# A float32 feature network on one core: six raw slots in place of four, six steps opened by halves, side work cut small

## The reference, cut to what matters

```python
# features (1024, 2, 5128), stm (1024, 2, 1), W_ft (512, 5128), b_ft (512,),
# W1 (32, 1024), b1 (32,), W2 (1, 32), b2 (1,), all float32
w = jnp.einsum('bpf,mf->bpm', features, W_ft) + b_ft
l1_x = jnp.clip(stm * w, 0.0, 1.0).reshape(features.shape[0], -1)
l2_x = jnp.clip(l1_x @ W1.T + b1, 0.0, 1.0)
return l2_x @ W2.T + b2
```

## Time and profile before

| | us |
|---|---|
| median of 3 runs | 432.38 |
| the three runs | 429.82, 432.38, 434.44 |
| the profiled execution, its own time | 432.02 |
| its span, first to last instruction | 430.2 |

### The profile page before, as it was taken

One profiled execution on the slowest core, in us unless ns is written; L12 is line 12 of the kernel. 1 busy time (PEld: TensorE's weight loads), 2 busy tenths in 40 slices (PEclk: granted clock), 3 DMA queues, 4 the chain that ended last, 5 costly groups with the idle time before them and its releaser, 6 DMA issues.

```text
span 430.2 us, 4578 instructions
## 1 busy us (share of the span) xinstructions
PE 407.0 (95%) x1756; PEld 323.3 (75%) x1756; DVE 349.6 (81%) x321; ACT 196.2 (46%) x176; POOL 13.2 (3%) x32
## 2 busy tenths in 40 slices
PE   6969999979999989998999999999999899999995
PEld 4747777858777868786878888878788778888862
DVE  3887888896899989979899877897887975698625
ACT  4464454343448444424444674363444448444300
POOL 2090000000000000000000000000000000000000
PEclk9999999989999999998999999999999999999999
DMA  7999797876867666663666766658667766778200
GB/s 237 387 239 269 219 267 247 253 226 200 264 227 244 223 233 235 244 226 143 244 245 244 240 222 237 240 205 337 239 235 238 240 194 195 240 231 254 96 2 0
DMA packets 27300, 96.37 MB, mean 224 GB/s; under 512 B 3432, under 2 KB 6384, under 8 KB 22032
## 3 DMA queue, kind: packets, MB, share of 16 engines
q1 hardware_dynamic: 26656, 95.44, 66.9%
q0 software_dynamic: 624, 0.66, 0.8%
HBM read 96.08 MB, written 0.00 MB: 223 GB/s over the span
## 4 chain that ended last, share of the span: by engine, by line
PE 65%; DMA 15%; DVE 12%; issue 5%; SPq 2%; ACT 1%; DVEq 0%
PE sums L496 63%; DMA xs<-x_p 15%; DVE x_lo L400 5%; DVE w_lo L397 1%; DVE xs L374 1%; PE sums L554 1%; PE sums L598 1%; DVE ws L378 1%; DVE x_lo L352 1%; DVE c_all L413 1%; ACT x_hi L275 0%; SPq L209 0%; DVE c_all L477 0%; DVE ws L364 0%; DVE xr L454 0%
## 5 line engine op out<-in xcount | busy, mean ns | idle before, releaser
L496 PE MATMUL sums<-x_lo,w_hi 128*128 128x512 f32 x560 | 178.0, 396 | 13.8 <-DVE x_lo L400 13.6
L496 PE MATMUL sums<-x_hi,w_hi 128*128 128x512 f32 x560 | 178.0, 396 | 3.2 <-ACT x_hi L264 2.3
L496 PE MATMUL sums<-x_hi,w_lo 128*128 128x512 f32 x560 | 177.2, 395 | 0.2 <-DVE w_lo L347 0.2
L289 ACT ACTIVATE x_hi<-xs 128x2048 fp32r<-128x2048 f32 x67 | 128.7, 1921 | 79.6 <-DVE xs L384 34.9
L400 DVE TENSOR_TENSOR x_lo<-xs,x_hi 128x2048 fp32r<-128x2048 f32 x67 | 153.0, 2284 | 0.0
L496 PEld LDWEIGHTS sums<-x_lo,w_hi 128*128 128x128 f32 x560 | 104.9, 190 | 42.2 <-issue 21.0
L496 PEld LDWEIGHTS sums<-x_hi,w_hi 128*128 128x128 f32 x560 | 106.4, 191 | 29.2 <-ACT x_hi L264 2.8
L496 PEld LDWEIGHTS sums<-x_hi,w_lo 128*128 128x128 f32 x560 | 106.8, 191 | 23.5 <-DVE w_lo L347 0.6
L284 ACT ACTIVATE w_hi<-ws 128x512 fp32r<-128x512 f32 x67 | 42.5, 634 | 116.9 <-PE sums L496 42.1
L397 DVE TENSOR_TENSOR w_lo<-ws,w_hi 128x512 fp32r<-128x512 f32 x67 | 45.9, 684 | 14.7 <-DMA ws<-w_p 14.7
L384 DVE TENSOR_TENSOR xs<-xs 128x2048 f32<-128x2048 f32 x20 | 45.8, 2288 | 8.0 <-DMA xs<-x_p 8.0
(11 more groups left out here) (59 smaller groups left out, 88.7 us busy)
## 6 DMA issues: line engine op xcount, KB each, us to landing
xs<-x_p SPq DMA_DIRECT2D x40, 1024.0 KB, 5.6
xs<-x_p SPq DMA_DIRECT2D x57, 512.0 KB, 5.6
ws<-w_p SPq DMA_DIRECT2D x43, 256.0 KB, 3.2
ws<-w_p SPq DMA_DIRECT2D x17, 384.0 KB, 3.4
ws<-w_p SPq DMA_DIRECT2D x20, 128.0 KB, 4.1
open_x<-x_p SPq DMA_DIRECT2D x2, 512.0 KB, 6.9
stm_all<-stm SPq DMA_DIRECT2D x1, 1024.0 KB, 7.5
open_x<-x_p SPq DMA_DIRECT2D x2, 256.0 KB, 3.8
```

Source lines behind the costliest of these rows:

```text
L289: nc.scalar.activation(x_hi[:, g % HI, :, :], x_pair(g), ACT.Copy).then_inc(x_hi_ready, 1)
L496: return nc.tensor.matmul(sums[:, bank, :], w[:, wslot, wpos, m * P:(m + 1) * P], x[:, xslot, xpos, c * BANK:(c + 1) * BANK], start=start, ...
```

## The change

- `RAW` 4 becomes 6. Slots 0 to 3 lie where they lay (`RAW_HOME`). Slots 4 and 5 of `xs` lie, until step 40 (`TURN`), in 4 x 4 KB per partition that later hold blocks 2 and 3 of `c_all` (`c_late`), and from step 40 on in the first four kept `x` blocks, whose last use is step 43. The raw area of `ws` shrinks from three to two blocks per slot, as the third block of pass 0 is now loaded straight to its kept place, by a DMA of its own (`s_loaded`).
- Loads of steps up to 39 and from 46 on wait for step g - 6; those of steps 40 to 43 for step g - 4 as before; those of 44 and 45 for `x_sum`, so for the kept blocks to have been read.
- `OPEN` 3 becomes 6: steps 3, 4 and 5 are also made by halves, from their normal slots; three steps are still staged (`STAGED`). Of the opening, `open_low(5, 2, 1)` moves ahead of `sums_of(3)`.
- `WARM_UP` 8 becomes 16.
- Rest: the two memsets and the small DMAs of POOL come after three steps in place of two (and none of the two memsets at the start); L454's two and L457 go from g = 12 to g = 12, 14 and 16.
- `combine` and the multiplications of `finish` go by 128x1024, at g = 45, 46, 48, 49 and 54, 55, with the clip at g = 57. In the fourth pass they are also cut, at the same g as before.

The core of the diff (renames and pure re-indexing left out):

```diff
-WARM_UP = 8
+WARM_UP = 16
-OPEN = 3
-RAW = 4
+STAGED = 3
+OPEN = 6
+RAW = 6
+RAW_HOME = 4
-OPEN_HALVES = ((0, 0), (1, 0), (0, 1), (2, 0), (1, 1), (2, 1))
+OPEN_HALVES = ((0, 0), (1, 0), (0, 1), (2, 0), (1, 1), (2, 1), (3, 0), (3, 1), (4, 0), (4, 1), (5, 0), (5, 1))
+TURN = 2 * K_PAIRS
...
+        c_early = sb("c_early", [P, 2, 2 * COLS])
+        c_late = sb("c_late", [P, 2, 2 * COLS], at=xs_at + 4 * CST * COLS)
...
+        def slot(g):
+            return g % RAW if g < TURN else (g - TURN) % RAW
+        def raw_x(g):
+            n = slot(g)
+            if n < RAW_HOME:
+                return 2 * n
+            return (CST if g < TURN else TST) + 2 * (n - RAW_HOME)
...
-            for g in range(OPEN, STEPS):
+            for g in range(STAGED, STEPS):
                 f, k = pass_of(g)
-                if g >= RAW:
+                if g in (TURN + RAW_HOME, TURN + RAW_HOME + 1):
+                    sp.wait_ge(x_sum, TURN + 2 * (g - TURN - RAW_HOME + 1))
+                elif TURN <= g < TURN + RAW_HOME:
+                    sp.wait_ge(step_done, g - RAW_HOME + 1)
+                elif g >= RAW:
                     sp.wait_ge(step_done, g - RAW + 1)
                 if f == 0:
-                    sp.dma_start(ws[:, i:i + 3, :], w_p[k, :, 0:3, :]).then_inc(w_loaded[n], 16)
+                    sp.dma_start(ws[:, i:i + 2, :], w_p[k, :, 0:2, :]).then_inc(w_loaded[n], 16)
+                    sp.dma_start(ws[:, KEPT + k, :], w_p[k, :, 2, :]).then_inc(s_loaded[n], 16)
...
-            pool.memset(xr_raw[:, :], 0.0).then_inc(rest_zeroed, 1)
-            pool.memset(wr_raw[:, :, :], 0.0).then_inc(rest_zeroed, 1)
...
-            pool.wait_ge(step_done, 2)
+            pool.wait_ge(step_done, STAGED)
+            pool.memset(xr_raw[:, :], 0.0).then_inc(rest_zeroed, 1)
+            pool.memset(wr_raw[:, :, :], 0.0).then_inc(rest_zeroed, 1)
...
             def open_half(n, g, pos):
+                if g >= HI:
+                    sc.wait_ge(step_done, g - HI + 1)
...
                 if g == K_PAIRS + 2:
+                    sc.wait_ge(rest_ready, 3)
                     drain(0)
...
             sums_of(2)
+            open_low(5, 2, 1)
+            for g in range(STAGED, OPEN):
+                sums_of(g)
+                open_low(2 * g, g, 0)
+                open_low(2 * g + 1, g, 1)
             sums_of(OPEN)
-            open_low(5, 2, 1)
...
-                if g == third + 5:
-                    combine(3, c_all[:, 2, :], 1, 16)
-                if g == third + 8:
-                    dve.wait_ge(c_sum, 1)
-                    combine(3, c_all[:, 1, :], 2, 16)
-                if g == third + 16:
-                    finish(3, 1, 2)
+                for m in range(2):
+                    cols = slice(m * COLS, (m + 1) * COLS)
+                    if g == TURN + 5 + m:
+                        combine(3, m, c_all[2][:, cols], 16)
+                    if g == TURN + 8 + m:
+                        dve.wait_ge(c_sum, m + 1)
+                        combine(3, m, c_all[1][:, cols], 16)
+                    if g == TURN + 14 + m:
+                        scale(3, 1, m, m + 3)
+                if g == TURN + 17:
+                    clip(3, 6)
```

More of the change, by code:

```diff
@@ L114, in feature_net @@
         t_loaded = [sem(f"t_loaded{j}") for j in range(RAW)]
-        open_w_loaded = [sem(f"open_w_loaded{j}") for j in range(OPEN)]
-        open_x_loaded = [sem(f"open_x_loaded{j}") for j in range(OPEN + 1)]
+        s_loaded = [sem(f"s_loaded{j}") for j in range(RAW)]
+        open_w_loaded = [sem(f"open_w_loaded{j}") for j in range(STAGED)]
+        open_x_loaded = [sem(f"open_x_loaded{j}") for j in range(STAGED + 1)]
         open_hi = sem("open_hi")
@@ L351, in open_low @@
                     dve.wait_ge(open_hi, before + 2 + i)
-                    nc.vector.tensor_tensor(x_lo[:, g, pos, a:b], x_src[:, a:b],
-                                            x_hi[:, g, pos, a:b].bitcast(F32), ALU.subtract)\
+                    nc.vector.tensor_tensor(low_x(g)[:, pos, a:b], x_src[:, a:b],
+                                            x_hi[:, g % HI, pos, a:b].bitcast(F32), ALU.subtract)\
                         .then_inc(open_lo, 1)
@@ L466, in _ @@
+                if g == TURN + 17:
+                    clip(3, 6)
                 if g == fourth + 2:
-                    combine(1, xs[:, TST:TST + 2, :].rearrange("p m n -> p (m n)"), 5, 24)
+                    for m in range(2):
+                        combine(1, m, xs[:, OUT + m, :], 24)
                 if g == fourth + 3:
-                    finish(1, 1, 5)
+                    for m in range(2):
+                        scale(1, 1, m, m + 7)
+                    clip(1, 10)
                 if g == fourth + 4:
-                    combine(2, xs[:, TST + 2:TST + 4, :].rearrange("p m n -> p (m n)"), 8, 24)
+                    for m in range(2):
+                        combine(2, m, xs[:, OUT + 2 + m, :], 24)
@@ L472, in _ @@
                 if g == fourth + 5:
-                    finish(2, 0, 8)
+                    for m in range(2):
+                        scale(2, 0, m, m + 11)
+                    clip(2, 14)
             for b in range(4):
@@ L494, in _, with product, operands @@
         def _(pe):
-            def product(bank, w, wslot, wpos, x, xslot, xpos, m, c, start, stop=False):
-                return nc.tensor.matmul(sums[:, bank, :], w[:, wslot, wpos, m * P:(m + 1) * P],
-                                        x[:, xslot, xpos, c * BANK:(c + 1) * BANK], start=start, stop=stop,
-                                        skip_group_check=True)
+            def product(bank, w, x, m, c, start, stop=False):
+                return nc.tensor.matmul(sums[:, bank, :], w[:, m * P:(m + 1) * P], x[:, c * BANK:(c + 1) * BANK],
+                                        start=start, stop=stop, skip_group_check=True)
+            def operands(g, wpos, xpos):
+                return (w_hi[:, g % HI, wpos, :], w_lo[:, slot(g), wpos, :],
+                        x_hi[:, g % HI, xpos, :], low_x(g)[:, xpos, :])
             def open_products(n, g, pos):
@@ L506, in open_products @@
                         for m in range(2):
-                            product(m * 2 + c, w_hi, 0, 0, x_hi, 0, 0, m, c, True)
+                            product(m * 2 + c, wh, xh, m, c, True)
                     pe.wait_ge(open_lo, 1)
@@ L510, in open_products @@
                         for c in range(PERSP):
-                            product(m * 2 + c, w_lo, 0, 0, x_hi, 0, 0, m, c, False)
+                            product(m * 2 + c, wl, xh, m, c, False)
                     for c in range(PERSP):
@@ L514, in open_products @@
                         for m in range(2):
-                            product(m * 2 + c, w_hi, 0, 0, x_lo, 0, 0, m, c, False)
+                            product(m * 2 + c, wh, xl, m, c, False)
                     return
@@ L519, in open_products @@
                     for c in range(PERSP):
-                        product(bank + m * 2 + c, w_hi, g, pos, x_hi, g, pos, m, c, g == 0)
+                        product(bank + m * 2 + c, wh, xh, m, c, g == 0)
                 pe.wait_ge(open_lo, before + 1)
@@ L523, in open_products @@
                     for c in range(PERSP):
-                        product(bank + m * 2 + c, w_lo, g, pos, x_hi, g, pos, m, c, False)
+                        product(bank + m * 2 + c, wl, xh, m, c, False)
                 pe.wait_ge(open_lo, before + 2)
@@ L527, in open_products @@
                     for c in range(PERSP):
-                        mm = product(bank + m * 2 + c, w_hi, g, pos, x_lo, g, pos, m, c, False)
+                        mm = product(bank + m * 2 + c, wh, xl, m, c, False)
                 if pos == 1:
@@ L549, in step @@
                                 pe.wait_ge(drained, 8 * (f - 1) + b + 1)
-                            product(b, w_hi, h, wpos, x_hi, h, xpos, m, c, start)
+                            product(b, wh, xh, m, c, start)
                             if last and f < PASSES:
-                                product(b, w_hi, h, wpos, x_lo, r, xpos, m, c, False)
+                                product(b, wh, xl, m, c, False)
                                 if (f, bank) in REST:
@@ L557, in step @@
                                         skip_group_check=True)
-                                mm = product(b, w_lo, r, wpos, x_hi, h, xpos, m, c, False, stop=True)
+                                mm = product(b, wl, xh, m, c, False, stop=True)
                                 if not (n == 1 and m == 1 and c == PERSP - 1):
@@ L566, in step @@
                         for c in range(PERSP):
-                            product(bank + m * 2 + c, w_hi, h, wpos, x_lo, r, xpos, m, c, False)
+                            product(bank + m * 2 + c, wh, xl, m, c, False)
                         for c in range(PERSP):
-                            mm = product(bank + m * 2 + c, w_lo, r, wpos, x_hi, h, xpos, m, c, False)
```

(8 more changed lines are left out.)

172 lines of the change are left out of this document (96 added, 76 removed).

## The result

The changed kernel takes 413.67 us (median of 4 runs, 413.17 to 414.66) against 431.1 (4 runs): a ratio of 0.963, 95% interval 0.955 to 0.971. The forecast was 412.7, in a range of 408 to 419.5. Its profiled execution took 413.34 us, span 411.6, mean granted clock 0.992.

What follows compares the result with a forecast made beforehand. PE was held up by late x loads; step 6 resuming at 45.0, 345.0 of matmuls, slow spell 1.7, steps 40 to 43 0.5, near misses 0.5, tail 18.2 gave span 410.9, plus 1.8 around it 412.7 us; range 408 to 419.5.

Steps and rivals of the forecast that it cites:

- slow spell: PE at half speed after the wait at step 6: 1.7 us lost, two of three earlier spells gone.
- steps 40 to 43: Loads there still look ahead by four; cost taken as 0.5 us, between 0 and 3.
- near misses: PE waits of 0.1 to 0.3 us, 3.5 in all before; 3.0 removed, 0.5 left in the sum.
- Late loads bound it, and the lead cures it: Steps 7 to 69: six slots release loads 10.9 us earlier, removing nine PE waits (12.0 us); bounds 0 and 18.5.
- Side work at nothing: Rest's pieces and halves of combine and finish cost nothing against VectorE's lead of 6.5 us.
- Without it each would be late: Without the 6.5 us lead, each piece of VectorE's side work would be 1.2 us late.
- The wait moves from step 3 to step 6: Opening: PE's 3.04 us wait at step 3 becomes 2.4 us at the change from halves to whole steps.
- POOL now starts over 3 us later, so 0: Opening: step 7's data, in at 40.6 and wanted at 40.3, cost nothing despite POOL's small DMAs.
- rival 2: Opening short of data if 268 GB/s is a ceiling; step 7 in at 44.8, total 417 us; chance 0.14.
- Warm-up 0: Opening: doubling the warm-up matmuls is worth 0, as the half step at 13.66 waits for data; bounds -1.8 and +1.7.
- Rivals 3 and 5: 3: VectorE bounds pass 1, 416 us, chance 0.11; 5: six steps' loads hinder each other, 441 us, chance 0.03.
- rival 4: The waits stay, by SP's order or a lead that never fills: 431.5 to 432 us; chance 0.03.

Runs made afterwards that it cites:

- both edits: Changed kernel with POOL's memsets and small DMAs after step 7 and step 6 in the order of the opened halves; 409.15 us.

## Why the prediction was right

Its terms against the profile after:

| term | forecast | measured |
|---|---|---|
| step 3 begins | 25.8 | 25.05 |
| PE stands at step 6 until | 45.0 | 46.08 |
| its wait | 2.4 | 4.1 |
| slow spell | 1.7 | 1.7 |
| steps 40 to 43 | 0.5 | 0 |
| near misses | 0.5 | 0 |
| tail | 18.2 | 18.7 |
| span | 410.9 | 411.6 |

The span is closer than its terms, and that is partly luck: the two cautions of 0.5 that came to nothing cover most of the 1.1 by which step 6 goes on late. Without them the sum would have been 409.9. One of its signs was missed: the granted clock is 0.992 and not 0.995 or more, because of the tail.

- **Late loads bound it, and the lead cures it.** Shown by taking the look-ahead alone back: all of the gain goes. That run also shows the weak side of my working: 10.9 us expected, 17.8 found. I had added up the waits of before; late loads also lengthen the wait of the opening and the slow spell behind it (6.1 us of half speed in place of 3.4).
- **Side work at nothing.** Shown by the run with whole blocks: 0.3 us, within the noise. "Without it each would be late" is shown too, by the two runs with a look-ahead of four.
- **The wait moves from step 3 to step 6.** Right in place and mechanism (sums, sums, low part on VectorE), mis-sized by 1.7. The step that failed is "POOL now starts over 3 us later, so 0". The forecast's own sum had the load of step 7 in at 40.6, VectorE was ready for it at 39.8, and it came at 41.5: the stretch of 199 GB/s lay on the loads up to step 7, and VectorE stood idle for 1.8 us. VectorE idle for data before 45 us was the forecast's sign of rival 2, and that rival was there in small, by POOL's small DMAs and not by a ceiling of 268 GB/s: 20 to 26 moved at 400. Putting the small DMAs off gave about the forecast's own wait. PE goes on 1.1 later than forecast; the other 0.6 of the 1.7 is PE's earlier start, which costs nothing.
- **Slow spell behind it:** right; where the longest wait is 1.4 us (both edits), the granted clock is 1.00.
- **Steps 40 to 43:** four waits of VectorE for `x`, 7.5 us together, and one of 3.1 for `w`, all inside the lead; 0 on PE. My 0.5 was caution.
- **Warm-up 0:** right, by the run with eight. The rule that sustained matmuls release the clock (the Trainium skill, TensorE: Matmul & The Clock Gate, Part 1: The HAM clock gate) agrees with both: the first two products take 0.75 us behind sixteen and 1.22 behind eight, though the record of the granted clock says 1.00 for 0 to 10 us in both. It buys nothing where data end the wait. The 1.8 us put on it does not follow from its rows, which give 5.3 - 12 x 0.2267 = 2.6; the first 12 products took 3.64, so 1.7 less.
- **Rivals 3 and 5** did not come: VectorE held its lead through pass 1 (the chain's 787 matmuls), and the DMA rate with loads looking ahead by six was 400 GB/s outside POOL's small DMAs.
- **The chances** add up to 1.01, and rival 4 has 0.04 in one place and 0.03 in the other.

Open: when exactly the `x` load of step 7 lands. With POOL's small DMAs early, six steps by halves and a look-ahead of six, VectorE waited 1.7 to 2.2 us for it in four profiles and not at all in two (eight warm-up matmuls, step 6 reordered); with a look-ahead of five it waited 0.4. In the three profiles with the small DMAs late it never waited. So the small DMAs are a cause, but not the only one, and the 1.6 us of the look-ahead of five can't be put down to it.

## What to carry to other kernels

Where loads come "just in time" on the median, every slower one is a stall, and each pause may bring a spell of half speed on top. Count the time from the freed slot to the last operand made of it, in steps. One step of slack over that did here all that two did, with the side work in small pieces; that one step would also hide it whole was not tried. Two steps hid side work in blocks of up to 3.7 us, which without them cost some 4 us in all. Then look at changes of rhythm (halves to whole steps) and at small DMAs beside the big ones, and order the consumer's work so that what is made last is used last.

## What the runs showed of the hardware

Small DMAs on POOL's queue halve what is moved in all (199 against 400 GB/s over the same stretch at the same DMA share of 1.04), though they are 0.66 MB; put off, they took the low rate with them (201 over 62 to 68).

Waits of 2.2 to 7.4 us in the opening were followed by a spell of half speed in all profiles but one, where the wait was 2.4 us (the run with eight warm-up matmuls). In the kernel before, a wait of 1.9 us was followed by one and a wait of 2.1 us was not, as the next matmuls show (PE by time, and the stretches behind them):

```profile
196.82 0.70 PE L496 MATMUL sums<-x_lo,w_hi 128*128 128x512 f32 x2 [1.89 <-DVE x_lo L400]
...
198.66 1.06 PE L496 MATMUL sums<-x_lo,w_hi 128*128 128x512 f32 x2
...
345.10 0.70 PE L496 MATMUL sums<-x_lo,w_hi 128*128 128x512 f32 x2 [2.06 <-DVE x_lo L400]
...
346.54 0.61 PE L496 MATMUL sums<-x_lo,w_hi 128*128 128x512 f32 x2
```

```profile
196.00:202.00 6.00, 5.18 (x16) 4.16 (x17) 5.82 (x5) 2.54 (x2) 0.00 (x0) 0.72 0.54 206
344.00:350.00 6.00, 4.90 (x22) 4.10 (x23) 6.00 (x7) 2.65 (x3) 0.00 (x0) 1.00 0.71 210
```

So the length of a pause alone does not settle whether it brings a slow spell.
